# Self attention with the second value half in key tile 1 and the second key half in tile 2, the keys' rope and parts moved one or two tiles later

## What is computed

```python
def _attn(xq, ctx, wq, wkv, wo, bo):
    q = _heads(xq @ wq)
    k, v = jnp.split(ctx @ wkv, 2, axis=-1)
    ...
    q = _rope(q, sq, cq)
    k = _rope(k, sk, ck)
    sim = jnp.einsum('bhnd,bhmd->bhnm', q, k) * DH ** (-0.5)
    a = jax.nn.softmax(sim, axis=-1)
    o = jnp.einsum('bhnm,bhmd->bhnd', a, v)
    o = o.transpose(0, 2, 1, 3).reshape(xq.shape[0], xq.shape[1], MID)
    return o @ wo + bo

attn_in = _adaln(x, cond, ln1_w, ln1_b, g1_w, g1_b, b1_w, b1_b)
x = _attn(attn_in, attn_in, sa_wq, sa_wkv, sa_wo, sa_bo) + x
```

## Time and profile before

| | |
|---|---|
| median of 3 runs | 2160.61 us (2159.16 to 2161.61) |
| profiled execution | 2168.07 us |
| its span, first to last instruction | 2166.3 us |
| TensorE busy | 2051.1 us, 95% |
| VectorE busy | 1754.4 us, 81% |
| ScalarE busy | 1426.4 us, 66% |
| mean granted TensorE clock | 0.975 |

### The profile page before, as it was taken

The page is one execution under the profiler, slowest core; times in us unless marked ns, Lnnn a source line. Parts: engine busy times, 40 slices in busy tenths (PEclk is TensorE's granted clock), DMA queues, the critical chain, the costliest instruction groups (busy, mean ns, idle before and its releaser), DMA issues. The chain is left out here.

```text
span 2166.3 us, 40686 instructions
## 1 busy us (share of the span) xinstructions
PE 2051.1 (95%) x16360; PEld 921.0 (43%) x16360; DVE 1754.4 (81%) x2723; ACT 1426.4 (66%) x1838; POOL 18.1 (1%) x16
## 2 busy tenths in 40 slices
PE   4799999999999999999999999999887999996999
PEld 2333333345333334533333543333622444454676
DVE  6899899986999998699999779987688888835654
ACT  4587778774787776677787567786367666623452
POOL 3000000000000000000000000000000000000000
PEclk8799999999999999999999999999999999987999
DMA  6010111011211110111010012111323343424111
GB/s 202 30 40 31 61 39 41 31 64 36 65 36 40 50 50 31 51 50 60 31 50 31 31 50 79 40 50 50 112 91 92 108 124 119 129 74 114 39 40 40
DMA packets 99282, 135.42 MB, mean 63 GB/s; under 512 B 34501, under 2 KB 72343, under 8 KB 99095
## 3 DMA queue, kind: packets, MB, share of 16 engines
q1 hardware_dynamic: 99095, 132.83, 18.6%
HBM read 67.29 MB, written 13.11 MB: 37 GB/s over the span
## 5 line engine op out<-in xcount | busy, mean ns | idle before, releaser
L713 ACT ACTIVATE sa_probs<-sa_ps_s 128x1024 f32<-128x1024 f32 x512 | 496.3, 1022 | 131.0 <-PE sa_ps_s L490 130.9
L505 PE MATMUL sa_ps_o<-sa_probs,sa_v_pair 128*64 128x512 f32 x2048 | 531.4, 609 | 1.4 <-DVE sa_mx L895 1.4
L908 DVE TENSOR_TENSOR sa_acc<-sa_acc,sa_probs 128x1024 f32<-128x1024 f32 x384 | 452.7, 1220 | 19.9 <-ACT sa_probs L713 11.9
L895 DVE CUSTOM_DVE_ANT_0 sa_rise<-sa_ps_t,sa_rise 128x512 f32<-128x512 f32 x504 | 327.3, 687 | 123.3 <-PE sa_ps_t L467 123.3
L483 PE MATMUL sa_ps_s<-scores_or_weights 64*128 64x512 f16 x3072 | 375.5, 377 | 0.9 <-ACT raw_or_keys L687 0.9
L701 ACT ACTIVATE sa_rise<-sa_ps_t 128x1024 f32<-128x1024 f32 x252 | 257.4, 1021 | 141.1 <-PE sa_ps_t L460 139.7
L483 PEld LDWEIGHTS sa_ps_s<-scores_or_weights 64*128 64x128 f16 x3072 | 151.9, 94 | 156.1 <-ACT sa_v_pair L692 6.8
L505 PEld LDWEIGHTS sa_ps_o<-sa_probs,sa_v_pair 128*64 128x64 f32 x2048 | 116.0, 135 | 150.0 <-issue 127.2
L460 PE MATMUL sa_ps_t<-sa_kd,scores_or_weights 64*128 64x512 f16 x504 | 99.3, 390 | 18.5 <-ACT scores_or_weights L697 7.0
L460 PEld LDWEIGHTS sa_ps_t<-sa_kd,scores_or_weights 64*128 64x128 f16 x504 | 25.1, 93 | 200.2 <-issue 162.3
L467 PE MATMUL sa_ps_t<-scores_or_weights 64*128 64x512 f16 x504 | 98.1, 385 | 11.3 <-ACT sa_rise L701 11.2
(11 more groups left out here) (322 smaller groups left out, 3643.6 us busy)
## 6 DMA issues: line engine op xcount, KB each, us to landing
sa_swp<-raw_or_keys SPq DMA_DIRECT2D x124, 256.0 KB, 2.4
sa_inv<-sa_scratch SPq DMA_DIRECT2D x128, 128.0 KB, 2.9
ca_swp<-raw_or_keys SPq DMA_DIRECT2D x64, 256.0 KB, 2.4
ca_inv<-ca_scratch SPq DMA_DIRECT2D x64, 256.0 KB, 3.9
sa_xs<-in_x SPq DMA_DIRECT2D x4, 1024.0 KB, 5.9
sa_xr<-in_x SPq DMA_DIRECT2D x4, 1024.0 KB, 7.0
x_after_cross<-scores_or_weights SPq DMA_DIRECT2D x32, 128.0 KB, 2.0
ff_xr<-x_after_cross SPq DMA_DIRECT2D x4, 1024.0 KB, 6.1
```

The source lines that it names most:

```text
L505: ins = pe.matmul(ps_o[rows(x), half(c)], v_pair[:, kt, rows(x)], probs[:, kt % 2, c, half(x)], start=(kt == 0), stop=(kt == NK - 1))
L713: act.activation(probs[:, kt % 2, c, :], ps_s[c][:, :], ACT.Exp, scale=float(DH) ** -0.5).then_inc(s_p, 1)
L895: dve.tensor_tensor_reduce(out=larger, in0=max_banks(j, t)[:, half(x)], in1=larger, scale=1.0, scalar=-3.0e38, op0=ALU.add, op1=ALU.max, a ...
L908: dve.tensor_tensor(acc[:, c, :], before, probs[:, kt % 2, c, :], ALU.add).then_inc(s_acc[c], 1)
```

## The change

K_AT becomes (0, 2) and V_SECOND 1: in tile 1 TensorE projects the second half of the values, in tile 2 the second half of the keys. Every user of these names moves with them: the waits of `differences`, the copies on ScalarE.

| work (group) | tile before | tile after |
|---|---|---|
| `high` of the queries (g + 2), ScalarE | 1 | 2 |
| `low` of the queries (g + 2), VectorE | 1 | 2 |
| `multiply` of the keys (g + 2), VectorE | 2 | 3 |
| `rotated` of the keys (g + 2), VectorE | 3 | 5 |
| `high` of the keys (g + 2), ScalarE | 5 | 6 |
| `high_output` half 0 (g - 1), ScalarE, not in 9, 17, 25 | 6 | 5 |
| `low_output` half 0 (g - 1), VectorE | 6 | 7 |
| `spread_inverses` (g - 1), SyncE | behind the swap of the keys | ahead of it |

```diff
-    K_AT, Q_AT = (0, 1), (3, 5)
-    V_FIRST, V_SECOND = NK - 1, 2
+    K_AT, Q_AT = (0, 2), (3, 5)
+    V_FIRST, V_SECOND = NK - 1, 1
...
+                if g >= 1:
+                    spread_inverses(g - 1)
                 if g + 2 < G:
                     swap(g + 2, 0)
-                if g >= 1:
-                    spread_inverses(g - 1)
...
-                    if kt == 1 and g + 2 < G:
+                    if kt == 2 and g + 2 < G:
                         high(g + 2, 1)
-                    if kt == 5 and g + 2 < G:
+                    if kt == 5 and g >= 1 and not late_norm(g):
+                        high_output(g - 1, 0)
+                    if kt == 6 and g + 2 < G:
                         high(g + 2, 0)
-                    if kt == 6 and g >= 1 and not late_norm(g):
-                        high_output(g - 1, 0)
...
-                    if kt == 1 and g + 2 < G:
+                    if kt == 2 and g + 2 < G:
                         low(g + 2, 1)
-                    if kt == 2 and g + 2 < G:
+                    if kt == 3 and g + 2 < G:
                         multiply(g + 2, 0)
-                    if kt == 3 and g + 2 < G:
+                    if kt == 5 and g + 2 < G:
                         rotated(g + 2, 0)
...
-                    if kt == 6 and g >= 1 and not late_norm(g):
-                        low_output(g - 1, 0)
                     if kt == 7 and g + 2 < G:
                         low(g + 2, 0)
                     if kt == 7 and g >= 1:
-                        if late_norm(g):
-                            low_output(g - 1, 0)
+                        low_output(g - 1, 0)
                         low_output(g - 1, 1)
```

## The result

The changed kernel takes 2197.45 us (median of 4 runs, 2192.45 to 2199.2), the kernel before 2161.11 in the runs beside it: ratio 1.0165, 95% interval 1.0146 to 1.0184. It is slower, by 36 us where 33 were forecast, and the time lies in the range (2178 to 2214). The profiled execution took 2199.2 us with a span of 2197.4.

The account below looks back on a forecast made before the run. TensorE was taken as the bound, VectorE second with little slack for its maxima. Class terms 6.7 + 12.0 + 8.4 + 5.0 + 0.9 = + 33 us, giving 2194 against the median 2160.6; range 2178 to 2214.

Parts of the forecast that it names:

- The walk through a plain group: Group 14, tiles 3 to 7: late key rope and the wait for the divide delay VectorE's maxima; 1.11 us lost.
- M of tile 4: Start of the first of tile 4's two maxima (L895) on VectorE, forecast at 733.8 in the earlier trace's times.
- D of tile 6: Start of tile 6's differences matmul (L460) on TensorE, forecast at 741.12, + 0.57 us against before.
- rival C: Value tile's 0.31 us excess comes from VectorE's full tile 2, so the move saves it: 2149 us, chance 0.05.
- Plain, statistics and Newton groups: Late maxima at the ends of tiles 4 to 6 cost 1.11, 2.4 and 2.1 us per group respectively.
- Transposing groups: Ten groups with transposes in tiles 4 and 6: maxima late by 0.15, then 0.34, together 0.5 us each.
- Group 29: No query projections and TensorE already waiting for VectorE there, so all added work shows: 2.8 us.
- Group 0: `multiply` leaves tile 2: maxima 1.14 us earlier, plus half of the slow-clock stretch's 1.7 us; in all - 1.9.
- the output groups: Groups 9, 17, 25, with output projections in tiles 1 to 6 and their late `high_output` kept: 0 us.
- Rival A: TensorE's clock also falls behind new gaps at tile 6's end, 1.7 us in 15 groups: 2220 us, chance 0.07.
- one sign of being wrong: The forecast would be wrong if TensorE's granted clock fell inside the groups.
- Rival B: VectorE absorbs the late work, for instance catching up in tile 6; only group 0's gain stays: 2159 us, chance 0.08.

Follow-up runs that it names:

- both doses: The kernel before with `key_differences` repeated in tile 5 of groups 0 to 29, once (2167.6 us, 1.0022) and three times (2212.19 us, 1.0228).
- the triple dose: The kernel before with three extra `key_differences` on VectorE in tile 5 of groups 0 to 29: 2212.19 us, ratio 1.0228.

## Why the prediction was right

**The walk through a plain group** held step by step. Its times plus 13.2 us, against group 14:

| step | forecast | measured |
|---|---|---|
| M of tile 4 | 747.0 | 746.92 |
| M of tile 5 | 751.1 | 751.01 |
| projection of tile 5 | 751.83 | 751.76 |
| exponentials of tile 5 | 751.7 | 751.66 |
| D of tile 6 | 754.32 | 754.22 |
| M of tile 6 | 757.54 | 757.45 |
| D of tile 7 | 758.89 | 758.81 |

Both constants of the earlier trace rows came again in this place: 1.36 us from late maxima to D (757.45 to 758.81), 0.75 to a projection. `multiply` started right behind the sums, never behind the swap. The value half costs 0.3 us more than a key half in either place: from rises to rises 5.62 against 5.32, in tile 2 before and in tile 1 after. So the excess is not VectorE's, which ends rival C. (From D to D the value tile went from 5.63 to 5.79, but a key tile in tile 1 also took 5.49 that way and not 5.32: by this count tile 1 is 0.17 longer with either half.)

**Classes.** Plain, statistics and Newton groups came within 0.06 us of their terms. Transposing groups were mis-sized by 0.14 each (1.4 in all): the 0.15 put down for tile 4 did not come (5.03 us before and after), the 0.34 did, and ScalarE's wait in tile 6, 0.31, was left out. Group 29 was mis-sized by 0.4, which no run takes apart.

**Group 0** gained 3.15, not 1.9, and not only where I looked. I had shortened the wait for the maxima by 1.14 and counted half of the slow stretch. Its TensorE timeline after, answering to the earlier trace rows:

```profile
96.96 0.41 PE L55 MATMUL sa_ps_t<-xT_hi,sa_wq_hi 128*64 128x512 f16 x2 [1.21 <-DVE sa_mx L895]
```

The wait went from 2.04 to 1.21 us, and the clock did not fall there (1.00 in 96 to 103 us, above): the other half of the 1.7 was saved too. Tile 3 takes 2.45 us less. The rest of the sum was not forecast. Tile 1 takes 1.51 less, from rises to rises: before, the queries' `high` (L697) waited 1.39 us for the rotation, ahead of tile 1's exponentials and of the copy of the projection, and D stood 1.45 us for that copy. With the query parts in tile 2 this wait is gone. Tile 2 is 0.30 shorter without the value half, tile 4 is 0.72 longer behind the late `multiply`, and tiles 0 and 6 are 0.39 longer together. So the query parts, costed at 0, had a share in group 0's gain; with them back in tile 1 the group gains by another path (tile 3 has no such wait then). The rows before:

```profile
83.15 1.06 ACT L697 ACTIVATE scores_or_weights<-raw_or_keys 128x1024 f16<-128x1024 f32 x1 [1.39 <-DVE raw_or_keys L878]
...
88.56 0.39 PE L460 MATMUL sa_ps_t<-sa_kd,scores_or_weights 64*128 64x512 f16 x2 [1.45 <-ACT raw_or_keys L687]
```

**The missed step** is the output groups, which I put at 0 because their output parts stay late. In tile 3 of group 9, VectorE:

```profile
505.74 1.22 DVE L873 TENSOR_TENSOR raw_or_keys<-raw_or_keys,ropeC 128x1024 f32<-128x1024 f32 x1
506.87 1.22 DVE L874 TENSOR_TENSOR sa_swp<-sa_swp,ropeS 128x1024 f32<-128x1024 f32 x1
508.01 0.41 DVE L928 SCALAR_TENSOR_TENSOR sa_xr<-sa_ps_t,sa_xr 128x256 f32<-128x256 f32 x1
```

and TensorE:

```profile
508.57 0.39 PE L460 MATMUL sa_ps_t<-sa_kd,scores_or_weights 64*128 64x512 f16 x2 [0.33 <-DVE sa_xr L928]
```

`residual` (L928) reads the output projection and is queued behind `multiply`, so TensorE waits 0.33 us for it. Before, the two met in tile 2, where the late `residual` cost 0.12, as the run with `residual` first shows (8.45 to 8.32). In tile 3 it costs 0.40 (8.05 to 8.45). The value half takes its 0.28 with it from tile 2 to tile 1 (8.05 to 8.32 there). So the group loses 0.40 less 0.12, the +0.27 of the table.

Group 17 loses 0.48 more in tile 3 (8.93), and the trace shows why: it is the second group of a layer norm as well, and ScalarE loads a function table there (1.28 us), so that the exponentials, the sums, `multiply` and `residual` all come late. The same load stood there before, and cost nothing then. ScalarE, VectorE and TensorE in group 17:

```profile
876.52 1.28 ACT L713 ACT_TABLE_LOAD   x1
```

```profile
878.87 2.36 DVE L908 TENSOR_TENSOR sa_acc<-sa_acc,sa_probs 128x1024 f32<-128x1024 f32 x2 [0.57 <-ACT sa_probs L713]
```

```profile
883.99 0.39 PE L460 MATMUL sa_ps_t<-sa_kd,scores_or_weights 64*128 64x512 f16 x2 [0.81 <-DVE sa_xr L928]
```

That the total came within 3 us of the forecast is luck in part, for the errors cancel: +1.4 (transposing), +1.3 (output), +0.4 (group 29), -1.3 (group 0), -0.3 (group 30).

**Rival A** (the clock falls in the new gaps) did not decide the time, but it did happen once. Groups 14 and 10 are at 1.00 with 0.75 and 1.98 us of TensorE idling in each, and took what the walk without a fall gives. In group 29, which has a Newton step too, TensorE's wait at the end of tile 4 grew from 0.92 to 2.06 us, and the granted clock behind it is 0.51, near the 1.2 GHz level:

```profile
1453.99 0.39 PE L460 MATMUL sa_ps_t<-sa_kd,scores_or_weights 64*128 64x512 f16 x2 [2.06 <-DVE sa_mx L895]
```

```profile
1454.80:1458.30 3.50, 3.50 (x20) 0.98 (x16) 3.32 (x7) 2.10 (x3) 0.00 (x0) 0.51 0.00 0
```

```profile
1464.55 0.39 PE L460 MATMUL sa_ps_t<-sa_kd,scores_or_weights 64*128 64x512 f16 x2 [0.85 <-DVE sa_mx L895]
```

So one sign of being wrong that the prediction named, a fall inside a group, did come, in one group of 30. It cost next to nothing there: two tiles later TensorE waits 0.85 us for VectorE again (1464.55), and VectorE's and ScalarE's work up to those maxima had not waited for the slow matmuls by more than about 0.1 us. The prediction had read only the short wait of this group (0.20) and not the 0.92. By the rule of the Trainium skill that the prediction named (TensorE: Matmul & The Clock Gate, section "A second HAM failure mode: psum-queue depth-cycling") the groups should have swung to the half clock again and again. One fall in self attention behind group 0 is all that this trace has. **Rival B** falls with the wait at 758.81: the maxima stand ahead of the sums.

## What to carry to other kernels

When two engines are both nearly full, cost a move by walking tile by tile to the one instruction that the other engine waits for, and compare its time with the room that this tile leaves. A comparison of sums of work misleads: here it gives 0.1 us where 1.1 were lost. Long work belongs in the tile behind which the other engine has most work of its own that needs nothing; look also at what is queued behind the moved work (here `residual`), and take every block in the middle of a tile as a wait of its own, and see whether it waits for the first maximum or for both.

## What was not expected of the hardware

The length of a gap alone doesn't tell whether TensorE's clock falls. A gap of 2.04 us in group 0 was followed by 0.57 in the kernel before, and a fall followed the same gap in both doses; a gap of 2.05 or 2.06 us in group 29 was followed by a fall in the changed kernel, in the one with the key rope alone, and in those with the later `high_output` and the query parts back. But the kernel with the earlier rotation kept 1.00 behind its 2.06 us in group 29, and the triple dose kept it behind gaps of 1.14 to 1.33 us in most groups, of 1.90 in the statistics groups and of 2.52 at the end of tile 6 of group 29. What else decides stays open. The stretches around the 2.06 us of the earlier rotation and the 2.52 of the triple dose:

```profile
1456.00:1466.00 10.00, 6.50 (x44) 1.88 (x42) 9.80 (x19) 4.88 (x7) 0.00 (x0) 1.00 0.00 1
1474.00:1484.00 10.00, 7.47 (x69) 3.31 (x67) 9.97 (x17) 6.45 (x10) 0.00 (x0) 1.00 0.04 9
```

And the part behind self attention, which no edit touched, took from 682 to 692 us in single executions, more than the gain of group 0.
